# Two filling products, not all of the first item, ahead of the injections of n and z in a GRU step

## The reference, cut to what matters

```python
h = gelu(x2 @ ffn_w1 + ffn_b1)            # third layer, 256 -> 1024 -> 256
x = x + gate2 * (h @ ffn_w2 + ffn_b2)

def cell(h, x):                           # fourth layer, 128 steps, 16 rows of 256
    gi = x @ W_ih + b_ih                  # needs no state
    gh = h @ W_hh + b_hh
    i_r, i_z, i_n = jnp.split(gi, 3, axis=-1)
    h_r, h_z, h_n = jnp.split(gh, 3, axis=-1)
    r = sigmoid(i_r + h_r)
    z = sigmoid(i_z + h_z)
    n = tanh(i_n + r * h_n)
    h_new = (1.0 - z) * n + z * h
```

## Time and profile before

| | us |
|---|---|
| median of 3 runs | 1674.68 |
| lowest and highest | 1669.46, 1674.72 |
| the profiled execution | 1674.92 |
| its span, first to last instruction | 1673.2 |
| first r activation of the recurrence (step 0) | at 1349.92 |
| last step ends, about | at 1664 |
| mean granted TensorE clock over the span | 0.842 |

### The profile page before, as it was taken

The page is one execution under the profiler, slowest core; times in us unless marked ns, Lnnn a source line. Parts: engine busy times, 40 slices in busy tenths (PEclk is TensorE's granted clock), DMA queues, the critical chain, the costliest instruction groups (busy, mean ns, idle before and its releaser), DMA issues. The chain is left out here.

```text
span 1673.2 us, 47650 instructions
## 1 busy us (share of the span) xinstructions
PE 1382.7 (83%) x16714; PEld 1069.0 (64%) x16714; DVE 1220.5 (73%) x6967; ACT 837.1 (50%) x3144; POOL 314.5 (19%) x616
## 2 busy tenths in 40 slices
PE   6989984445599959995998978989896699999865
PEld 4468753334466646664667867888883477777755
DVE  3368779999999999999995235666664557666754
ACT  5669833332455555554553226666654544444322
POOL 2026601111211121112111012222221211111110
PEclk8989975555599969995999989999998798979755
DMA  2000020100023203320335688676711300000000
GB/s 96 0 1 3 2 89 27 52 27 2 2 96 109 90 14 103 109 90 8 107 111 189 193 254 242 195 214 174 214 26 51 89 2 3 3 15 3 15 16 15
DMA packets 102839, 127.65 MB, mean 76 GB/s; under 512 B 6108, under 2 KB 79432, under 8 KB 97352
## 3 DMA queue, kind: packets, MB, share of 16 engines
q1 hardware_dynamic: 101744, 122.20, 23.8%
q0 software_dynamic: 272, 2.10, 0.6%
q10 hardware_dynamic: 584, 0.31, 0.1%
HBM read 70.06 MB, written 54.53 MB: 74 GB/s over the span
## 5 line engine op out<-in xcount | busy, mean ns | idle before, releaser
L1020 PE MATMUL bank<-s_tanh_hi,coup_hi 128*128 128x16 f16 x2048 | 136.6, 176 | 151.6 <-ACT s_tanh_hi L1010 150.3
L1020 PEld LDWEIGHTS bank<-s_tanh_hi,coup_hi 128*128 128x128 f16 x2048 | 91.4, 102 | 253.3 <-ACT s_tanh_hi L1010 248.8
L918 POOL TENSOR_SCALAR s_p_scaled<-s_p 128x32 f32<-128x32 f32 x128 | 37.4, 292 | 570.3 <-DVE s_p L901 550.6
L1010 ACT ACTIVATE s_tanh_hi<-s_s 128x32 f16<-128x32 f32 x256 | 58.8, 230 | 161.7 <-DVE s_s L835 158.4
L1532 ACT ACTIVATE prob<-bank,neg_max 128x128 f32<-128x128 f32 x256 | 90.5, 366 | 95.3 <-DVE neg_max L1572 95.3
L1020 PE MATMUL bank<-s_tanh_lo,coup_hi 128*128 128x16 f16 x2048 | 135.8, 176 | 2.3
L1020 PE MATMUL bank<-s_tanh_hi,coup_lo 128*128 128x16 f16 x2048 | 127.3, 171 | 0.0
L664 PE MATMUL bank<-x_hi,w_hi 128*128 128x512 f32 x256 | 120.3, 470 | 0.0
L1596 DVE TENSOR_TENSOR o_lo<-bank,o_hi 128x512 fp32r<-128x512 f32 x64 | 44.2, 691 | 91.5 <-ACT o_hi L1543 91.5
L1020 PEld LDWEIGHTS bank<-s_tanh_lo,coup_hi 128*128 128x128 f16 x2048 | 88.9, 101 | 31.6 <-DVE s_tanh_lo L829 1.1
L1818 PE MATMUL bank<-h_hi,w_h_hi 128*128 128x16 f16 x1536 | 91.4, 172 | 21.3 <-DVE h_hi L2038 21.1
(11 more groups left out here) (312 smaller groups left out, 4444.2 us busy)
## 6 DMA issues: line engine op xcount, KB each, us to landing
queries<-tile_stage SPq DMA_DIRECT2D x64, 256.0 KB, 2.3
keys<-tile_stage SPq DMA_DIRECT2D x64, 256.0 KB, 2.3
values<-tile_stage SPq DMA_DIRECT2D x64, 256.0 KB, 2.4
v<-values SPq DMA_DIRECT2D x64, 256.0 KB, 6.0
q_raw<-queries SPq DMA_DIRECT2D x10, 1024.0 KB, 9.9
k<-keys SPq DMA_DIRECT2D x10, 1024.0 KB, 12.1
x<-in_L_cond_qkv_w_dram SPq DMA_DIRECT2D x6, 1024.0 KB, 5.6
x<-queries SPq DMA_DIRECT2D x6, 1024.0 KB, 9.8
```

Source lines behind the costliest of these rows:

```text
L918: G.tensor_scalar(p_scaled, p, P_IN_P, None, MUL).then_inc(pool_done, 1)
L1010: A.activation(th_hi[:, :], s, ACT.Tanh, scale=scale).then_inc(hi_ready, 1)
L1020: ins = nc.tensor.matmul(coupled[:, B * m:B * m + B], w[:, o:o + P], th[:, B * c:B * c + B], start=(first and c == 0 and m == 0), stop=(la ...
```

## The change

A step whose first item has more than two products now issues two of them ahead of the injections of n and z, and the remaining ones behind them, ahead of what was behind them already. Transposes are left alone.

```diff
                 early, late = at[s][:1], at[s][1:]
+                if early and early[0][0] != "out" and early[0][4] - early[0][3] > 2:
+                    kind, n, m, lo, hi = early[0]
+                    early, late = [(kind, n, m, lo, lo + 2)], [(kind, n, m, lo + 2, hi)] + late
                 if s + 1 < T:
```

## The result

| | before | changed |
|---|---|---|
| median of 3 runs, us | 1674.68 | 1690.65 |
| lowest and highest | 1669.46, 1674.72 | 1688.42, 1696.81 |
| span of the profiled execution | 1673.2 | 1686.7 |
| mean granted clock | 0.842 | 0.831 |

The ratio is 1.0114, with a 95% interval from 1.0075 to 1.0154: slower by 16 us where 3.5 were forecast (1678.2 - 1674.7). On the chain the filling products have gone from 8% to 9% of the span, the recurrent ones stay at 7%.

What follows compares the result with a forecast made beforehand. Each step was taken as bound by PE's own work or, if later, the chain through ACT and DVE (2.30 us). Terms 1.5 + 0.7 + 1.1 = 3.3 us on 1674.9 gave 1678.2, range 1673.5 to 1682 us.

Steps and rivals of the forecast that it cites:

- (a): Injections of n and z, now two products behind that of r, might wait for ACT's z; costed at 0.
- each whole block that is cut pays 0.09 at full clock: Filling cut in two by the injections pays a second first-product gap; 1.5 us over 17 steps plus 0.7 over 8.
- [3]: Step with three filling products in one block ahead of the injections; at full clock bound by ACT and DVE, pays 0.
- [4]: Step with four filling products in one block ahead of the injections; at full clock under the 2.30 us chain, pays 0.
- [6]: Step with six filling products in one block ahead of the injections, PE-bound; 17 such steps, 1.5 us more.
- [5]: Step with five filling products in one block ahead of the injections; 8 at full clock, 0.7 us more.
- 0.14 a cut at half clock: A second block at half clock pays 0.57 - 0.43 us on PE; bounded by 0 and 0.57 a step.
- Eight steps pay at half clock: Steps 21, 22, 50, 51, 53, 57, 61 and 86, whole blocks at half clock, pay 1.1 us together.
- Rival 2: One more stretch of half clock, as in steps 65 to 74, adds 2.9 us: 1681.1 us; chance 0.14.
- 1: Rival: cutting a filling block costs nothing, as products cost the same wherever they stand: 1674.9 us; chance 0.12.
- 4: Rival: the injections wait after all, 0.15 us on 25 full-clock steps, 3.8 us more: 1682.0 us; chance 0.04.
- 3: Rival: a stretch of half clock goes, as filling runs up to the recurrent products, saving 2.9 us: 1675.3; chance 0.10.

Runs made afterwards that it cites:

- changed_again: The changed kernel once more, unaltered, in a later group beside its version with fifteen wasted products: ratio 1.0133 to before, 1681.82 to 1696.52 us.
- three_ahead: The changed kernel with three products ahead of the injections instead of two, cutting only first items of more than three: ratio 1.0089 to before, +15 us.
- cut_last: The change applied only in steps 86 to 93, where six first items are cut: ratio 1.0033 to before, +5.7 us; again 1.0037, +7.7 us.
- delay: The kernel before, with seven wasted products of 512 columns ahead of step 0: ratio 1.0027 to before, +4.4 us.

## Why the prediction was wrong

- *That the injections would not wait (a)*: right, 0.24 us behind the second product.
- *That each whole block that is cut pays 0.09 at full clock, and [3] and [4] nothing*: right. [6] pays 0.097, and [5] goes from 2.30 to 2.35 up to 2.40 to 2.43; [3] and [4] keep their periods, nearly all 2.30 to 2.32. Besides the gap of 0.08, the recurrent products start a little more slowly directly behind a filling product (1351.45 to 1351.66 for two groups, 0.21, against 0.19 before).
- *0.14 a cut at half clock*: too small, 0.20: step 53 takes 2.82 instead of 2.62. A late block of one pays the long gap too. Steps 52 and 54, [3] and [4] with transposes behind the injections, were put at nothing because they had a late item; they paid 0.11 and 0.12 (3.12 to 3.23, 3.54 to 3.66). PE in step 53, which answers to the earlier trace rows:

```profile
1483.94 0.77 PE L1746 MATMUL bank<-x_hi_b,w_hi 128*128 128x512 f32 x1
1484.51 0.63 PE L1746 MATMUL bank<-x_lo_b,w_hi 128*128 128x512 f32 x1
...
1485.11 0.77 PE L1746 MATMUL bank<-x_hi_b,w_lo 128*128 128x512 f32 x1
1485.69 0.32 PE L1818 MATMUL bank<-h_hi,w_h_hi 128*128 128x16 f16 x4
```

- *Eight steps pay at half clock*: the step that failed. The sum took the half-clock steps of the trace as given, and asked only what a cut costs in each. The cut decides how many there are: steps 61 to 65 and 86 to 93 were nearly all at half clock now, at 3.25 us where four products took 2.30 and 3.68 where five took 2.35 to 2.43, 0.95 to 1.3 us a step. That is 12.3 of the 16.8 us in this execution. In the shortest one (changed_again) the same term of the sum fails at other places: steps 19 to 24 and 50 to 58 took 2.5 us more each.
- *Rival 2, one more stretch for 2.9 us*: the right mechanism with the wrong place and size. The stretch of steps 65 to 74, at which it was to be read, stayed at full clock but for step 65; the stretches that were there already got longer. (In three_ahead steps 66 to 70 were at half clock.) I priced a stretch at 9.81 - 6.95 from steps that before left it soon, and bounded the number by one. That PE's work and idle time in a step stay almost equal was taken for evidence against it; cut_last shows a stretch grow from six cuts.
- *The other rivals*: 1 is out, since the cut blocks cost what was forecast; 4 too, since the injections follow after 0.24. Of 3 there is something: in changed_again steps 61 to 65 stayed at full clock, 0.9 us less than before, which the other stretches outweigh.
- *The comparison of three runs*: before also has executions of 1679.2 to 1682.9 us (9 of 61 in two later groups), at a mean granted clock of 0.839 to 0.844 where those below 1672 us have 0.845 to 0.849. That they have longer stretches is likely; no trace of one was kept. Three executions tell little of how often they come.

## What to carry to other kernels

Where TensorE runs at either clock, a change of order is to be priced at both, and the number of steps at half clock is a result of the change and not a given: look at what follows each fall of the clock, and put a length on it, not only a count. Read more than one execution: the same program can have its half-clock stretches in other places. Keep long products together: a break in a block costs its restart at once, and here half clock lasted longer with it. Where the clock is down, wasted products can give back more than they cost (1.0068 with them against 1.0133).

## What the runs showed of the hardware that was not expected

- PE recorded as busy 28.00 of 28.00 us, and granted 0.50 throughout (changed kernel, 1573 to 1601): the recorded busy time does not tell the clock.
- Fifteen more products made a kernel 9 us faster (1684.53 against 1693.30 in one group). Eight more seem to have made another one 5 us faster (1.0002 against 1.0033), with intervals that overlap.
- Seven products more ahead of the recurrence, and nothing changed in it, went with longer half-clock stretches in it: 316.82 us from the first to the last r activation instead of 314.04 (delay).
- Executions of one program differ by 15 us (1681.82 to 1696.52) with the mean granted clock from 0.837 to 0.825.
